# Weaving the third layer norm, the routing and the grouped experts of earlier batches into the attention turns

## What is computed

```python
h = _layernorm(x) * (1 + ca) + sa
x = x + ga * _L1_attn_ref(h, W_qkv, W_o)         # rope, causal, 16 heads of 8
h = _layernorm(x) * (1 + cb) + sb                # "third layer norm" below
x = x + gb * _L1_ffn_ref(h, ...)
# _L1_ffn_ref: route (sigmoid scores + bias, best 2 of 4 groups, best 4 of 16 experts, weights normed, times 2.5), then
g = einsum('th,eih->tei', x, gate_w); u = einsum('th,eih->tei', x, up_w)
h = silu(g) * u
yo = einsum('tei,ehi->teh', h, down_w)
routed = einsum('te,teh->th', combine, yo)
out = routed + mlp_shared(x)                     # one shared expert of 2 x 64
```

## Time and profile before

| | us |
|---|---|
| median of three runs | 2152.92 |
| the profiled execution's own time | 2167.51 |
| its span (first to last instruction) | 2165.8 |
| end of attention (last add to xT) | 1869.5 |
| end of third layer norm | 1897 |
| end of the last experts' add | 2154.5 |

### The profile page before, as it was taken

One profiled execution on the slowest core, in us unless ns is written; L12 is line 12 of the kernel. 1 busy time (PEld: TensorE's weight loads), 2 busy tenths in 40 slices (PEclk: granted clock), 3 DMA queues, 4 the chain that ended last, 5 costly groups with the idle time before them and its releaser, 6 DMA issues. The chain is left out here.

```text
span 2165.8 us, 24099 instructions
## 1 busy us (share of the span) xinstructions
PE 1745.6 (81%) x7317; PEld 854.3 (39%) x7317; DVE 1434.5 (66%) x1594; ACT 992.8 (46%) x1553; POOL 906.7 (42%) x507
## 2 busy tenths in 40 slices
PE   7788888888888898877838746878777788888998
PEld 5233333333333333332537633434443445543333
DVE  3099999999999999999432122656555556274444
ACT  3566666666656666663203322244343344441111
POOL 1277777777777777776250143011110010040000
PEclk8889999999999999999959955599898898987999
DMA  3112122212121222121014213221123220100001
GB/s 133 40 59 78 60 78 78 74 62 78 78 76 61 78 78 77 59 79 58 16 39 113 86 36 81 69 75 47 32 75 77 76 70 8 44 1 0 0 0 39
DMA packets 49081, 128.25 MB, mean 59 GB/s; under 512 B 5478, under 2 KB 36046, under 8 KB 39094
## 3 DMA queue, kind: packets, MB, share of 16 engines
q1 hardware_dynamic: 45782, 117.65, 17.0%
q0 software_dynamic: 3216, 9.51, 1.3%
HBM read 104.04 MB, written 23.01 MB: 59 GB/s over the span
## 5 line engine op out<-in xcount | busy, mean ns | idle before, releaser
L535 POOL TENSOR_TENSOR PR<-H,CS 128x1024 f32<-128x1024 f32 x256 | 601.9, 2356 | 202.5 <-DVE H L510 192.2
L510 DVE TENSOR_TENSOR_SCAN H<-DA,X 128x1024 f32<-128x1024 f32 x256 | 583.5, 2280 | 0.2
L433 PE MATMUL psY<-PR,W 128*128 128x512 f32 x1024 | 486.8, 598 | 1.1 <-POOL PR L535 1.1
L496 ACT ACTIVATE DA<-DT,negA 128x511 f32<-128x511 f32 x512 | 332.0, 711 | 96.0 <-DVE H L510 95.6
L503 DVE TENSOR_TENSOR X<-DU,psB 128x1024 f32<-128x1024 f32 x256 | 314.5, 1229 | 68.9 <-POOL DU L554 36.6
L433 PEld LDWEIGHTS psY<-PR,W 128*128 128x128 f32 x1024 | 193.7, 192 | 229.7 <-issue 215.2
L1222 ACT ACTIVATE a_PT<-a_psS 128x512 f32<-128x512 f32 x320 | 181.3, 601 | 156.5 <-PE a_psS L1126 152.9
L1270 DVE TENSOR_REDUCE a_MX<-a_psM 128x1 f32<-128x384 f32 (+3 forms) x352 | 206.8, 637 | 60.9 <-PE a_psM L1141 59.5
L413 PE MATMUL psB<-ST,sel 96*128 96x512 bf16 x256 | 100.4, 392 | 143.7 <-DVE X L503 143.6
L1140 PE MATMUL a_psM<-a_kst,a_qst 72*128 72x512 bf16 (+3 forms) x512 | 147.5, 336 | 35.1 <-DMA a_kst<-scratch_k 22.8
L1125 PE MATMUL a_psS<-a_qst,a_kst 75*128 75x512 bf16 (+3 forms) x512 | 138.4, 319 | 18.3 <-issue 17.0
(11 more groups left out here) (252 smaller groups left out, 2539.5 us busy)
## 6 DMA issues: line engine op xcount, KB each, us to landing
CS<-c_rows SPq DMA_DIRECT2D x64, 1024.0 KB, 4.6
scratch_q<-a_partsq SPq DMA_DIRECT2D x24, 384.0 KB, 3.6
a_qst<-scratch_q SPq DMA_DIRECT2D x8, 1152.0 KB
a_kst<-scratch_k SPq DMA_DIRECT2D x24, 384.0 KB
scratch_k<-a_partsk SPq DMA_DIRECT2D x8, 384.0 KB, 5.9
slots<-zeros POOLq DMA_DIRECT2D x1, 2624.0 KB, 10.1
stok<-slots SPq DMA_DIRECT2D x3, 768.0 KB, 7.2
work<-in_pack SPq DMA_DIRECT2D x1, 2272.0 KB, 9.6
```

What stands on the lines that cost most here:

```text
L433: last = nc.tensor.matmul(chunk(psY, c), w("ident"), chunk(PR[n % 4], c), start=False, stop=n == NS - 1)
L496: last = nc.scalar.activation(DA[:, s % 4, c, 1:T], chunk(DT[p], c)[:, 1:T], ACT.Exp, scale=negA[:, c * NS + s:c * NS + s + 1])
L510: nc.vector.tensor_tensor_scan(H[s % 4][:, :], DA[:, s % 4, :, :].rearrange("p c t -> p (c t)"), X[s % 2][:, :], 0.0, ALU.mult, ALU.add).t ...
L535: nc.gpsimd.tensor_tensor(both(PR[s % 4][:, :]), both(H[s % 4][:, :]), CS[q % 2][:, s % 4, :].unsqueeze(1).to_broadcast([P, NCH, T]), ALU. ...
```

## The change

The third layer norm and the routing of batch t-1, and the experts and the output of batch t-2, go into turn t of the attention, by one plan of slots that all engines sort (slot_plan: each piece has a place between 0 and 1 in its slot). Turn 0 is as before, turn 1 gets a layer norm and a routing, turns 2 to 7 all of it. last_experts_stage then does the experts of the last two batches, with the norm and the routing of the last one inside. layernorm_stage for the third norm, the two group stages and output_stage go.

In one turn the new pieces are: on PE the uses XC, VR, RB, LG, CP, OUT of the bank mb, and four products for each of nine chunks, G (gate), U (up), C (spread), D (down), where G, U and C share one bank, psE. ACT reads G twice, as half of it (GH, a Copy with scale 0.5) and as tanh of half of it (TH); GpSimd makes silu of them with a product and a sum; DVE multiplies by U, later by C. The banks of scores and of maxima go from three to two, the exponentials' buffers from four sets to three, the two causal mask products of one bank become one. All eight turns are written out, without a loop.

```diff
-        psM = [ps(f"psM{i}") for i in range(3)]
-        psS = [ps(f"psS{i}") for i in range(3)]
-        psO, mb = ps("psO"), ps("mb")
+        psM = [ps("psM0"), ps("psM1")]
+        psS = [ps("psS0"), ps("psS1")]
+        psO, mb, psE, psY = ps("psO"), ps("mb"), ps("psE"), ps("psY")
...
-        LATE = {3: ["G0"], 4: ["V"], 6: ["MA"]}
-        TAIL = ["F", "O"]
+        LATE = {2: ["XC"], 3: ["G0", "VR"], 4: ["V", "RB"], 5: ["LG"], 6: ["MA"], 9: ["CP"]}
+        TAIL = ["F", "O", "OUT"]
...
+        ROUTE_SLOTS = {6: ((0.3, 0), (0.8, 1)), 7: ((0.3, 2), (0.8, 3)), 8: ((0.3, 4), (0.8, 5))}
...
+            if t >= 2:
+                n = 9 * (t - 2) + CHUNKS[slot][0]
+                if slot < 9:
+                    plan += [(0.03, ("G", n)), (0.62, ("U", n)), (0.88, ("C", n))]
+                else:
+                    plan += [(0.03, ("G", n)), (0.35, ("U", n)), (0.5, ("C", n)), (0.55, ("G", n + 1)), (0.7, ("D", n)), (0.95, ("U", n + 1))]
+                if n % 9:
+                    plan.append((0.15, ("D", n - 1)))
...
+                return [("mb", t, "F"), ("mb", t, "O")]
+            return [("mb", t, "F"), ("D", 9 * (t - 2) + 8), ("mb", t, "O"), ("moe", t - 2), ("mb", t, "OUT")]
...
+            if what == "G":
...
+                elif c == 0:
+                    pe.wait_ge(HU_done, n)
+                else:
+                    pe.wait_ge(HC_done, RC * b + c)
+                nc.tensor.matmul(psE[:, :], w4("gate_w")[:, c * P:(c + 1) * P], h, start=True, stop=True).then_inc(G_ready, 1)
+            elif what == "U":
+                pe.wait_ge(TH_ready, n + 1)
+                nc.tensor.matmul(psE[:, :], w4("up_w")[:, c * P:(c + 1) * P], h, start=True, stop=True).then_inc(U_ready, 1)
+            elif what == "C":
+                pe.wait_ge(HU_done, n + 1)
...
+        def act_gate(act, n):
...
+            nc.scalar.activation(GH[:, :], psE[:, :], ACT.Copy, scale=0.5)
+            nc.scalar.activation(TH[n % 2][:, :], psE[:, :], ACT.Tanh, scale=0.5).then_inc(TH_ready, 1)
...
+        def dve_up(dve, n):
+            dve.wait_ge(U_ready, n + 1)
+            dve.wait_ge(SG_step, 2 * n + 2)
+            nc.vector.tensor_tensor(TH[n % 2][:, :], TH[n % 2][:, :], psE[:, :], ALU.mult).then_inc(HU_done, 1)
...
+            nc.gpsimd.tensor_tensor(h[:, :], h[:, :], GH[:, :], ALU.mult).then_inc(SG_step, 1)
+            pool.wait_ge(SG_step, 2 * n + 1)
+            nc.gpsimd.tensor_tensor(h[:, :], h[:, :], GH[:, :], ALU.add).then_inc(SG_step, 1)
...
+                sp.wait_ge(mb_used, use(t, "OUT") + 1)
+                sp.dma_start(out[(t - 2) * T:(t - 1) * T, :].rearrange("(k p) d -> p k d", p=P),
+                             OF[:, :].rearrange("p (k d) -> p k d", k=QT)).then_inc(stored, 16)
...
+                sp.dma_start(W4[:, :], pack4[:, 0:at]).then_inc(w4_loaded, 16)
```

More of the change, by code:

```diff
@@ L1057, in attention_stage @@
+        ROUTE_SLOTS = {6: ((0.3, 0), (0.8, 1)), 7: ((0.3, 2), (0.8, 3)), 8: ((0.3, 4), (0.8, 5))}
         SLOTS_T = range(2, PAIRS + 2)
-        def uses(more_p, more_m):
-            order = [x for slot in SLOTS_T for x in EARLY.get(slot, []) + LATE.get(slot, [])] + TAIL
[L1062 to L1070, removed]
+        CHUNKS = {slot: (slot - 2,) if slot < 9 else (7, 8) for slot in SLOTS_T}
@@ new lines, in wanted, with uses, use @@
+        def wanted(t, name):
+            if name in PRO:
+                return t + 2 < B
+            if name in ("V", "MA", "MB"):
+                return t + 1 < B
+            if name in ("XC", "VR", "RB", "LG", "CP"):
+                return t >= 1
+            return t >= 2 if name == "OUT" else True
+        def uses(t):
+            order = [x for slot in SLOTS_T for x in EARLY.get(slot, []) + LATE.get(slot, [])] + TAIL
+            return [x for x in order if wanted(t, x)]
+        def use(t, name):
+            return BEFORE + sum(len(uses(s)) for s in range(t)) + uses(t).index(name)
@@ new lines, in slot_plan, with add @@
+        def slot_plan(t, slot):
+            plan = []
+            def add(tags, lo, hi):
+                for n, tag in enumerate(tags):
+                    plan.append((lo + (hi - lo) * (n + 0.5) / len(tags), tag))
+            ahead = slot >= PAIRS
+            if not ahead or t + 1 < B:
+                add([("S", t + ahead, slot - PAIRS * ahead, u) for u in range(5)], 0, 0.55 if slot % 2 == 0 else 0.9)
+            if slot % 2 == 0:
+                add([("V", t, slot // 2 - 1, i) for i in range(QT)], 0.55, 1)
+            early = [("mb", t, x) for x in EARLY.get(slot, []) if wanted(t, x)]
+            half, a, b = M_SLOTS[slot] if slot in M_SLOTS and t + 1 < B else (0, 0, 0)
+            maxima = [("M", t + 1, half, g) for g in range(a, b)]
@@ L1074, in slot_items @@
                 early, maxima = early[1:], maxima[2:]
[L1075 to L1090, removed]
@@ new lines, in pe_maxima @@
+        def pe_maxima(pe, t, half, g):
+            j, h0, nh = groups(half)[g]
+            n = 2 * NG * t + half * NG + g
+            if n >= 2:
+                pe.wait_ge(M_used, n - 1)
+            wide = (j + 1) * P
+            for x in range(nh):
+                at = (h0 + x) * T
+                piece = psM[g % 2][:, x * wide:(x + 1) * wide]
+                nc.tensor.matmul(piece, qst[t % 2][0:72, at + j * P:at + (j + 1) * P], kst[t % 2][0:72, at:at + wide], start=True, stop=False)
+                last = nc.tensor.matmul(piece[:, j * P:wide], identb[:, :], mqk[:, :], start=False, stop=True)
+            last.then_inc(M_ready, 1)
@@ L1146, in pe_values @@
+        def pe_values(pe, t, g, i):
             if i == 0:
```

1024 lines of the change are left out of this document (564 added, 460 removed).

## The result

The changed kernel took 2253.65 us, the kernel before beside it 2152.22 us: a ratio of 1.048, 95% interval 1.0452 to 1.0507. It is slower by 101 us where +18 was forecast, and lies outside the range. The profiled execution has a span of 2250.2 us.

What follows compares the result with a forecast made beforehand. PE was taken to bound the attention turns, DVE their slots 6 to 8 after the change, with full turns of 99 us. Terms 3 + 16 + 173.7 + 41.5 + 80 - 296.3 gave +18, 2170 us; range 2112 to 2215.

Steps and rivals of the forecast that it cites:

- The loss to the lower clock is put at 0.5: Term of a full attention turn: PE's work at the lower clock adds 0.5 us to the 99 us.
- PE's waits in the turn: PE's idle time in a full turn: 3.5 us in slots 2 to 5, 11.5 in 6 to 8, 4.8 behind.
- the bound of slots 6 to 8: Slots 6 to 8 of a full turn: DVE sets 38.5 us against PE's 27, and is over 85% busy.
- The fourth rival (the clock): Turns with many short waits run at mean clock 0.80, +11 us a turn, 2230 us in all; chance 0.07.
- prologue and turn 0: Start of the attention: W4's 1.8 MB goes ahead of the first maxima's round trip, +3 us (0 to 8).
- Turn 7: Last attention turn, without maxima: a chunk's chain through psE, 7 to 8 us, sets 73 us instead of 31.5.
- The chunks: Nine expert chunks in a full turn, 3.09 us of PE work each, 27.8 us.
- Table loads, row against rule: ACT's four table loads a turn cost 1.28 us each by the trace; the skill's rule says 2.66 a switch.
- the third rival: Table switches cost 2.66 us, delaying exponentials in slots 4 and 6: some 2.5 us a turn, 2188 in all; chance 0.04.
- The wait for the stacked heads: PE's 9.2 us wait in slot 2 goes, gone or under 2 us from turn 3, left in turns 1 and 2.
- The last stage: Experts of the last two batches, with norm and routing of the last one: 80 us, wrong if over 8 away.
- The first rival (faster): Idle time in the attention turns is eaten: turns of 90 us, 2126 in all, deciding from 95.4 a turn; chance 0.29.

## Why the prediction was wrong

The direction was the likeliest of the three, the size was far off. By its own steps:

- **"The loss to the lower clock is put at 0.5": this is the term that failed.** PE's 502 matmuls take 80.7 us at a clock of 1.00 (the row above; another order, the same matmuls) and 93.3 in the changed kernel. So the term measures 12.6 us a turn. With the waits filled 7.2 of 8.8 us came back in the turn, and between the last two windows shown 4.8 of the turn for 4.7 of PE's work, so most or all of it counts. A turn of 113.0 is then 80.7 of work, 12.6 of clock and 19.7 not busy; the forecast of 99 was 79, 0.5 and 19.8 (3.5 in slots 2 to 5, 11.5 in slots 6 to 8, 4.8 behind). The clock explains 12.1 of the 14 us, PE's own work 1.7. The low clock itself came with the waits, and these with the bursts, so both went together when the order was changed.
- **PE's waits in the turn** were right in sum, 19.7 for 19.8, and even in slots 6 to 8, 11.5 for 11.5, but by luck, not for the reason given. DVE was not the bound of slots 6 to 8: at 70% busy it missed the 85% that I named. The waits come from DVE's order, as single steps instead of bursts show, and that no term had. The routing steps themselves ran at 0.25 us from start to start, as I took them, and GpSimd held DVE up by about the 4 us that I took: by the lengths of the steps 3.8 us of routing, of which leaving out the silu products gave back 3.0 net.
- **The fourth rival (the clock)** had the right mechanism with a chance of 0.07. Its 2230 us lies near the 2253.65 in part by luck. It put the mean at 0.80 and so 17 us of lost work a turn; the mean was 0.86 and the lost work 12.6. It then counted 11 of the 17, because most of the loss would lie under DVE's slots. Little was hidden: 7.2 of 8.8 us came back. DVE waits for U from PE (16.3 us a turn), so a slower PE makes DVE late; this is how I read it, no run isolates it. What I held against it, that the turns before had 0.86 to 0.95 with one long wait each, was evidence for it: where PE never waited, the same rows have 1.00. The Trainium skill, "TensorE: Matmul & The Clock Gate", section "A second HAM failure mode: psum-queue depth-cycling", tells of a bf16 kernel in which short idle times between groups of products, while PE goes round its PSUM banks, bring the lower level back. The trace of this kernel, bf16 and fp32, agrees: 0.86 with the waits, 0.97 with them filled.
- **The banks** were missing from the sum. Two instead of three cost 0 to 7 us a turn, 2.7 in the mean, and 12.1 in prologue and turn 0, even without routing or chunks: 31 us over the attention. In the full turns this is contained in the clock and the waits above. In prologue and turn 0 it is the miss: +13.4 for +3, outside the 0 to 8 that I allowed.
- **Turn 1** took 86.5 for 81: a clock of 0.80 and 5.4 us of waits for maxima, without a chunk; the two were not taken apart there.
- **Turn 7** took 82.3 for 73. "The chain of a chunk through psE sets it" is not borne out: PE was busy 65.4 of the 82.3 us, and 2.2 us less in each chunk's chain took 3.1 us of its waits but did not shorten the turn, at a lower clock. With the factor multiplied last and the clock at 0.98 PE was busy 60.5 us and the turn took 72.8. How much of the miss is chain and how much is clock is not separated.
- **The chunks** cost in a full turn nearly what I gave them, 27.7 for 27.8, but between turns at unlike clocks (0.86 and 0.78); that the numbers meet is in part luck.
- **Table loads, row against rule:** the row was right, the third rival false. Of four loads in the turn three are followed by their activation 0.01 or 0.02 us later, and the fourth waited for PE:

```profile
1788.87 1.28 ACT L1410 ACT_TABLE_LOAD   x1
1790.16 0.60 ACT L1410 ACTIVATE a_TH<-a_psE 128x512 f32<-128x512 f32 x1
...
1809.14 1.28 ACT L1396 ACT_TABLE_LOAD   x1
1810.44 0.22 ACT L1396 ACTIVATE a_scores<-a_mb 128x64 f32<-128x64 f32 x1
```

- **The wait for the stacked heads** went as told, a turn earlier: 2.4 us are left in turn 1, none from turn 2 on. Slot 9 and the tail took 16.2 for 16.8.
- **The last stage** took 75.5 for 80, within the 8 that I allowed; W4's transfer did not delay the prologue (from its first VectorE instruction to the first maximum 39.4 us, before 40.4).
- **The sums** have small slips that change nothing: the parts of a full turn add to 99.3, DVE's to 38.7, turn 7 was taken as 31.5 with 296.3 behind it where the earlier trace rows has 32.3 (0.8 us), and 11 us in each of six turns on 2170 is 2236, not 2230.
- **The first rival (faster)** needed turns under 95.4 us. The change as made was far from it, but the place was right: with the steps laid singly, the maxima spread, C earlier, the factor last and two handoffs apart, turns 2 to 5 are 90 to 96 us and the kernel is 1.0% faster than before. The change moved the work where it could be hidden; its order then gave more away than the hiding brought.

What stays open: why equal turns of one kernel alternate between two clocks, as in the last two windows shown, was not tried.

## What to carry to other kernels

When small steps of one engine are moved into another engine's schedule, ask how long each piece blocks that engine, and whether the banks between the two cover that long; the sum of its work says little while it is under the turn's length. Where the rows of a stage show the lower clock beside TensorE's waits, price the waits twice: the wait, and the work behind it at the lower clock, read from two windows of the same instructions. Read the price of fewer banks over all turns, since here single turns showed anything from 0 to 7 us. A cheap probe for the second part is to fill the waits with products of zeros onto a running sum, with the same products elsewhere as the control.

## What the runs showed of the hardware

- TensorE's lower clock took 12.6 of 113 us here, in turns with waits of up to 4.2 us. It fell inside waits of 4.2 and 2.3 us, and a turn whose longest wait was 1.6 us still had a mean of 0.95. Products that change nothing, 46 of them at 379 ns each (0.213 apart), held the clock at 0.97 and made the kernel 1.5% faster than without them (2220.88 for 2253.65).
- Leaving work out lowered the clock: without chunks, with 16.5 us of 85.3 not busy, it was 0.78; with them, 19.7 of 113.0 not busy, 0.86.
- GpSimd's two 128x512 operations for silu took 1.09 us each in the turns, its rotary one in the same turn (L1561) 1.27, and its product in the earlier trace rows 1.27; what decides is open:

```profile
L1573 POOL TENSOR_TENSOR a_TH<-a_TH,W 128x512 f32<-128x512 f32 x9 | 9.8, 1090 | 70.6 <-ACT a_TH L1410 70.6
L1575 POOL TENSOR_TENSOR a_TH<-a_TH,W 128x512 f32<-128x512 f32 x9 | 9.8, 1087 | 0.7
L1561 POOL TENSOR_TENSOR work<-work 128x512 f32<-128x512 f32 x2 | 2.5, 1268 | 0.0
```

- A routing step of 0.22 us that met a GpSimd operation of this size took up to 1.15 (the step at 1817.21 above met the rotary one of 1817.12, 1.15 us long); over a turn the routing lost 3.8 us so.
